# Placement of the experts' weights merged into routing, and parts of 16, 24 and 24 tiles

## What is computed

```python
logits = jnp.einsum('btd,ed->bte', x, gate_w) + expert_bias      # 12 experts
topk_logits, topk_idx = jax.lax.top_k(logits, TOP_K)             # TOP_K = 2
topk_w = jax.nn.softmax(topk_logits, axis=-1)
w = jnp.einsum('btk,btke->bte', topk_w, onehot)
w_zero = jnp.sum(w[..., E_FFN:], axis=-1)                        # experts 8 to 11 return x
h = jax.nn.silu(jnp.einsum('btd,efd->btef', x, w1))              # 8 experts, 256 -> 512
y = jnp.einsum('btef,edf->bted', h, w2)                          # 512 -> 256
out = jnp.einsum('bte,bted->btd', w_ffn, y) + w_zero[..., None] * x
```

## Time and profile before

| what | value |
|---|---|
| median of 3 runs | 2664.8 us |
| the profiled execution | 2638.58 us |
| its span | 2636.6 us |
| PE busy | 2485.2 us (94%) |
| DVE, ACT, POOL busy | 1906.8, 1665.0, 767.3 us |
| routing, first to last instruction | 1967.9 to 2106.1 |
| placement | 2109.2 to 2146.1 |
| experts | 2146.5 to 2636.6 |
| output scatters (L1998) | 122 |

### The profile page before, as it was taken

The page is one execution under the profiler, slowest core; times in us unless marked ns, Lnnn a source line. Parts: engine busy times, 40 slices in busy tenths (PEclk is TensorE's granted clock), DMA queues, the critical chain, the costliest instruction groups (busy, mean ns, idle before and its releaser), DMA issues. The chain is left out here.

```text
span 2636.6 us, 47763 instructions
## 1 busy us (share of the span) xinstructions
PE 2485.2 (94%) x16108; PEld 1295.4 (49%) x16109; DVE 1906.8 (72%) x3228; ACT 1665.0 (63%) x2989; POOL 767.3 (29%) x896
## 2 busy tenths in 40 slices
PE   6987789999999999999999999999989779999998
PEld 4554223333333333333333333333338669989997
DVE  5887768888788887787887887878818655556543
ACT  1656347777777777777777777777765355545554
POOL 2545301121111111111211111111113747757644
PEclk8999779999999999999999999999999789999999
DMA  5698643242442432433424323321128457567565
GB/s 176 200 255 220 132 81 87 67 112 82 94 90 75 98 91 74 100 86 81 86 83 91 88 79 78 70 54 38 54 70 256 161 172 138 114 107 130 95 102 76
DMA packets 225081, 286.06 MB, mean 108 GB/s; under 512 B 29526, under 2 KB 178550, under 8 KB 224502
## 3 DMA queue, kind: packets, MB, share of 16 engines
q1 hardware_dynamic: 185596, 235.80, 35.6%
q0 software_dynamic: 32160, 41.57, 9.2%
q10 hardware_dynamic: 7136, 6.32, 0.7%
HBM read 143.64 MB, written 139.08 MB: 107 GB/s over the span
## 5 line engine op out<-in xcount | busy, mean ns | idle before, releaser
L240 DVE TENSOR_REDUCE mxc<-ps 128x2 f32<-128x1024 f32 (+4 forms) x1168 | 1298.0, 1149 | 316.2 <-PE ps L228 165.8
L1188 ACT ACTIVATE probs<-ps 128x512 f32<-128x512 f32 (+1 forms) x2240 | 1177.6, 588 | 462.2 <-PE ps L1145 450.6
L1161 PE MATMUL ps<-probs,vs 128*32 128x512 f32 (+3 forms) x5120 | 599.7, 541 | 1.3 <-POOL probs L1078 1.2
L1145 PE MATMUL ps<-qs,ks 99*128 99x512 bf16 (+3 forms) x1760 | 504.5, 352 | 14.0 <-DMA qs<-m_t 9.2
L228 PE MATMUL ps<-ks,qs 96*128 96x512 bf16 (+3 forms) x1760 | 464.5, 354 | 25.2 <-DVE mxc L240 17.4
L1078 POOL TENSOR_SCALAR_AFFINE_SELECT probs<-probs 128x512 f32<-128x512 f32 x256 | 161.7, 635 | 869.3 <-ACT probs L1188 869.3
L1145 PEld LDWEIGHTS ps<-qs,ks 99*128 99x128 bf16 x1760 | 147.5, 97 | 380.3 <-ACT probs L1188 271.7
L228 PEld LDWEIGHTS ps<-ks,qs 96*128 96x128 bf16 x1760 | 163.3, 99 | 178.8 <-DVE mxc L240 42.6
L1874 PEld LDWEIGHTS ps<-x_t,w_at 128*128 128x128 f32 x2000 | 245.1, 194 | 11.7 <-issue 5.6
L1874 PE MATMUL ps<-x_t,w_at 128*128 128x128 f32 x2000 | 246.6, 277 | 4.2 <-ACT x_t L1915 4.2
L1998 POOL DMA_INDIRECT out<-ys,idx x122 | 194.6, 1595 | 172.7 <-DMA out<-ys,idx 91.5
(11 more groups left out here) (172 smaller groups left out, 2206.4 us busy)
## 6 DMA issues: line engine op xcount, KB each, us to landing
ks<-k_parts SPq DMA_DIRECT2D x66, 256.0 KB, 4.2
qs<-q_parts SPq DMA_DIRECT2D x66, 256.0 KB, 4.1
xs<-slot_x SPq DMA_DIRECT2D x128, 131.0 KB, 2.2
v_ones<-vout SPq DMA_DIRECT2D x64, 256.0 KB, 3.6
vs<-v_ones SPq DMA_DIRECT2D x64, 256.0 KB, 3.2
attn_t<-o_sb SPq DMA_DIRECT2D x64, 256.0 KB, 2.8
slot_x<-zero SPq DMA_DIRECT2D x48, 262.0 KB, 2.5
q_parts<-parts SPq DMA_DIRECT2D x96, 128.0 KB
```

Of the source, the lines that this page charges most:

```text
L240: return dve.tensor_reduce(mxc[:, h0:h0 + nh, i, c], unit_view(ps, u, at), AX_X, ALU.max)
L1145: ins = pe.matmul(o[:, h, :], ks[r][0:SROWS + MROWS, h0 + h, j * P:(j + 1) * P], qs[r][0:SROWS + MROWS, h0 + h, J * QJ + lo:(J + 1) * QJ], ...
L1161: ins = pe.matmul(o_ps[SLOT * g:SLOT * (g + 1), lo:QJ], vs[:, r, j, SLOT * g:SLOT * (g + 1)], probs[:, (NKT * r + m) % NPB, g, 0:QJ - lo], ...
L1188: act.activation(probs[:, (NKT * r + m) % NPB, h0:h0 + nh, 0:QJ - lo], st_view(r, s), ACT.Exp, scale=DH ** -0.5).then_inc(exp_done, 1)
```

## The change

- `PARTS` is 16, 24, 24. NPAIR becomes 20, 28, 28, and part 0 lies in one batch, part 2 in two.
- `place` is gone. Its work stands in `route`'s lists: part 0's chain in steps 8 and 9, part 1's in steps 16 and 17, part 2's in steps 20 and 21 (its counts stand ahead of the transposes of expert 5), the transposes and copies of expert e in step 16 + e, the loads of experts 2 to 7 at the end of SyncE's list, the tile tables at the end of VectorE's.
- All chains share one set of buffers (`chain_buffers`); `positions` multiplies in place and reduces in two instructions. The counts of a later part wait until the one before is placed.
- POOL scatters in each of the last 8 steps of routing, two in the first four and three in the others, and then all the rest of part 0 and the first 6 tiles (`AHEAD`) of part 1. `later` of part 0 in the experts is shorter by these 6.
- `rbc` is one buffer, so the load of group t waits for the multiply of group t - 1.

```diff
-PARTS = [24, 24, 16]
+PARTS = [16, 24, 24]
-SCATTERING = 6
-EARLY = 14
+SCATTERING = 8
+AHEAD = 6
...
 class Chain:
-        self.sel, self.posf, self.slot = sb("sel", [P, 2, n, E]), sb("posf", [P, 2, n]), sb("slot", [P, 2, n])
+        self.posf, self.slot = (view(x, 2 * n, "p (c t) -> p c t", c=2) for x in ("posf", "slot"))
...
     def positions(self, dve, s, r, pos_done):
         for c in range(2):
-            s.mark(dve.tensor_tensor(self.sel[:, c, :, :], rank, self.oh[:, c, :, 0:E], ALU.mult))
+            s.mark(dve.tensor_tensor(self.oh[:, c, :, 0:E], rank, self.oh[:, c, :, 0:E], ALU.mult))
         s.wait()
-        s.link(dve.tensor_reduce(self.posf[:, :, :], self.sel[:, :, :, :], AX_X, ALU.add))
+        for c in range(2):
+            s.mark(dve.tensor_reduce(self.posf[:, c, :], self.oh[:, c, :, 0:E], AX_X, ALU.add))
+        s.wait()
...
 def route
-                        if t >= RAW + 2:
-                            sp.wait_ge(y_done, t - RAW - 1)
+                        if t > RAW:
+                            sp.wait_ge(y_done, t - RAW)
...
+                for e in range(2, E):
+                    for m in range(2):
+                        sp.wait_ge(wt_done, 4 * (e - 2) + 2 * (m + 1))
+                        load_weights(sp, a, w_in, w_ld, e, m)
...
+                def counts(*parts):
+                    def stage(t):
+                        for p in parts:
+                            if t == LASTS[p]:
+                                pe.wait_ge(oh_done, p + 1)
+                                if p > 0:
+                                    pe.wait_ge(pos_done, 2 * p)
+                                chains[p].counts(pe, r, bank).then_inc(cnt_mm, 1)
+                def weights(t):
+                    e = t - (NB - E)
+                    for half in range(4):
+                        m, h, n = half // 2, half % 2, 4 * e + half
+                        if h == 0:
+                            pe.wait_ge(w_ld[m][e % 2], 16 * (e // 2 + 1))
+                        if n == 0:
+                            pe.wait_ge(mid_done, NB)
+                        if n >= 4:
+                            pe.wait_ge(wt_copy, n - 3)
...
-                blocks((6, counts), (0, output), (3, logits), (2, normed))
+                blocks((6, counts(0, 2)), (8, counts(1)), (0, output), (3, logits), (8, weights), (2, normed))
...
-                blocks((2, scales), (3, shifted), (5, top2), (0, attended), (1, residual), (4, inverses), (4, table), (5, chosen), (6, placed), (9, zeros))
+                blocks((2, scales), (3, shifted), (5, top2), (0, attended), (1, residual), (4, inverses), (4, table),
+                       (5, chosen(0, 2)), (6, placed(0, 2)), (7, zeros), (7, chosen(1)), (8, placed(1)))
                 dve.wait_ge(topi_done, NB)
+                dve.wait_ge(mult_done, NB)
+                for p in range(NPARTS):
+                    tile_table(dve, s, r, p, cmp, eidf, last, turned)
...
-                blocks((1, deviation), (1, normalise), (2, normed), (5, shares))
+                blocks((1, deviation), (1, normalise), (5, shares(0, 2)), (8, shares(1)), (8, weights), (2, normed))
...
-                todo = [(t, c) for t in range(PARTS[0]) for c in range(2)]
+                todo = [(t, c) for t in range(PARTS[0] + AHEAD) for c in range(2)]
...
-                        for _ in range(3):
-                            scatter_row(pool, d, r, *todo.pop(0), scat)
+                        for _ in range(2 if t < NB - SCATTERING // 2 else 3):
+                            scatter()
                 blocks((0, modulate), (0, scatters))
-                while len(todo) > 2 * (PARTS[0] - EARLY):
-                    scatter_row(pool, d, r, *todo.pop(0), scat)
+                while todo:
+                    scatter()
+                scattered(pool, 0, scat[0])
...
-def place(nc, a, k, r, w, w_in, w_ld, d, ps, scat):
...
 def experts
-        later = [range(FIRST[p + 1], FIRST[p + 1] + PARTS[p + 1]) if p + 1 < NPARTS else range(0) for p in range(NPARTS)]
+        later = [range(FIRST[p + 1] + (AHEAD if p == 0 else 0), FIRST[p + 1] + PARTS[p + 1]) if p + 1 < NPARTS else range(0) for p in range(NPARTS)]
```

More of the change, by code:

```diff
@@ L1433, in route @@
         HK = H // KC
-        chain = Chain(ctx, nc, 0, PARTS[0])
+        bufs = chain_buffers(ctx, nc)
+        chains = [Chain(ctx, nc, bufs, p) for p in range(NPARTS)]
+        cmp, eidf = hn[:, :, :].rearrange("p j c -> p (j c)")[:, 0:HT * E].rearrange("p (t e) -> p t e", e=E), sb("eidf_all", [P, HT])
+        last, turned = sb("last", [P, 1]), sb("turned_at", [P, HT])
+        wt_done, wt_copy = sem("wtr"), sem("wtc")
         c_ld, cstep, oh_done, cnt_mm, pos_done, w_dif, w_sig = (sem(n) for n in ("c", "cstep", "oh", "cnt", "pos", "dif", "sig"))
@@ new lines, in placed, with stage @@
+                def placed(*parts):
+                    def stage(t):
+                        for p in parts:
+                            if t == LASTS[p]:
+                                dve.wait_ge(cnt_mm, p + 1)
+                                chains[p].ranks(dve, s, r, bank)
+                                chains[p].positions(dve, s, r, pos_done)
+                                dve.wait_ge(w_sig, p + 1)
+                                chains[p].extras(dve, s, r)
+                                dve.nop().then_inc(pos_done, 1)
+                                if p > 0:
+                                    chains[p].zero_weights(dve, s, r)
+                    return stage
@@ L1646, in normed, with shares, stage, weights @@
                     act.copy(h2_t[:, :, :, :], pd).then_inc(ht_done, 1)
[L1648 to L1653 removed]
+                def shares(*parts):
+                    def stage(t):
+                        for p in parts:
+                            if t == LASTS[p]:
+                                act.wait_ge(w_dif, p + 1)
+                                chains[p].shares(act, r, w_sig)
+                    return stage
+                def weights(t):
+                    e = t - (NB - E)
+                    if e < 0:
+                        return
+                    for half in range(4):
+                        m, h = half // 2, half % 2
+                        act.wait_ge(wt_done, 4 * e + half + 1)
+                        dst = w["w1t"][:, e, h, :] if m == 0 else w["w2t"][:, e, 2 * h:2 * h + 2, :].rearrange("p f c -> p (f c)")
+                        act.copy(dst, ps[:, half, :]).then_inc(wt_copy, 1)
+                blocks((1, deviation), (1, normalise), (5, shares(0, 2)), (8, shares(1)), (8, weights), (2, normed))
             @block.gpsimd
@@ L1775, in experts @@
-def experts(nc, d, k, r, w, zb, ps, out):
+def experts(nc, d, k, r, w, zb, ps, out, scat):
     with ExitStack() as ctx:
```

174 lines of the change are left out of this document (57 added, 117 removed).

## The result

The changed kernel takes **2679.64 us** (median of 10 runs, 2674.85 to 2683.0), the kernel before beside it 2665.96 (10 runs): ratio 1.0045, 95% interval 1.0033 to 1.0058. Between the medians lie 13.7 us (by the ratio 12.0), slower, and 2679.6 is outside the forecast range of 2651 to 2673. The profiled execution took 2674.85 us.

The account below looks back on a forecast made before the run. In the end of routing no engine is full, so the order of queues counts; TensorE fills the experts. Tail -11 and part 0 +9 give -2, with the first steps -2.5: 2664.8 to about 2662 us, range 2651 to 2673.

Parts of the forecast that it names:

- I work out the difference in the profiled execution and carry it over to the median.: Whole kernel: difference worked out on the 2638.6 us profiled execution, then applied to the 2664.8 us median, 26.2 above it.
- The term of the merged tail: End of routing with placement: VectorE's tile tables end it at 2134.9 instead of ScalarE's copy at 2146.1, 11 us gained.
- the single buffer of inverses: Routing steps 0 to 15: the load's wait costs nothing, 3 us as other bound; steps some 2.5 us earlier.
- The term of part 0: Experts: POOL sends part 1's rows too late for the shortened part 0, TensorE waits, 9 us lost.
- The budget of POOL: Part 0 of the experts: POOL's scatters, additions and waits sum to 124.7 us until the word for part 1.
- no loss, as now: Experts, change from part 1 to 2: POOL's word comes before TensorE ends, so nothing is lost.
- would be 25: Experts, part 0: the loss without the six tiles sent ahead, which save 15.5 us of POOL's queue.
- The tail at full clock: Rival, end of routing: transposes fill TensorE's pauses, full clock, end near 2128, 18 gained, total 2656; chance 0.24.
- POOL not late in part 0: Rival, experts: waits and scatters overlap better, loss 0 to 1 us, total 2654; chance 0.10.
- POOL's waits at even changes: Rival, part 0 of the experts: expert changes at even tiles also wait 2.65 us, 10.6 more, total 2673; chance 0.12.
- The weights ending the stage: Rival, end of routing: weight loads still end it, near 2142, only 4 us gained, total 2669; chance 0.12.
- the 0.18 for slower: Whole kernel: chance given to a time above 2670.1 us, mostly from late POOL waits and weights ending routing.

Follow-up runs that it names:

- e1: The kernel before, unchanged, run again for a second profile: 2668.1 us, ratio 1.0006.
- e8: The changed kernel, with POOL holding back the last 24 scatters of routing until ScalarE has copied the weights: 2689.4 us, ratio 1.0091.
- e5: The changed kernel with FLIGHT = 1, a tile's scatters waiting until the tile before has landed: 2685.1 us, ratio 1.0076.
- e6: The kernel before with FLIGHT = 1, a tile's scatters waiting until the tile before has landed: 2690.7 us, ratio 1.0091.
- e17: The kernel before with 24 row scatters repeated in part 2, on a chip with late signals: 2668.5 us, ratio 1.0031.
- e9: The kernel before with 24 row scatters repeated in part 2, on a chip without late signals: 2645.1 us, ratio 1.0021.
- e10: The kernel before, sending row scatters always two tiles in a pair, in groups of four, on a chip without late signals: 2650.4 us, ratio 1.0045.
- e13: The changed kernel, unchanged, on a chip without late signals: 2647.3 us, ratio 1.0032.
- e15: The kernel before with only routing and placement merged, old part sizes, on a chip without late signals: 2631.5 us, ratio 0.9972.
- e7: The changed kernel with 12 tiles of part 1 sent ahead in routing instead of 6: 2683.3 us, ratio 1.0068.
- e14: The kernel before with only the part sizes 16, 24, 24, on a chip without late signals: 2657.9 us, ratio 1.0073.
- e2: The changed kernel, unchanged, run again for a second profile: 2682.8 us, ratio 1.0058.
- e3: The kernel before with only the part sizes 16, 24, 24, on a chip with late signals: 2679.9 us, ratio 1.0043.
- e4: The kernel before with only routing and placement merged, old part sizes, on a chip with late signals: 2669.5 us, ratio 1.0013.

## Why the prediction was wrong

Forecast was -2.5 us, measured are +13.7. Of these 16.2 us about 5 come from late signals, 6 from terms of the sum that were mis-sized or put at nothing, and 5 are open.

**The first step that failed: "I work out the difference in the profiled execution and carry it over to the median."** The 26.2 us between them were read as a constant. By all that the runs show they were late signals: the profile has none and the time of the chips without them (2638.6; 2638 to 2640 in the runs above), the timed runs have the time of the others (2662 to 2666). And what e1 takes more than the profile of before lies only where POOL scatters rows: 10.8 us in the stage, then, from the first product with w2 to the last, 179.3 instead of 162.5 in part 0 and 172.1 instead of 170.2 in part 1; part 2, which scatters none, takes 117.6 in both. Each chip was seen at one time only, so whether it is lasting stays open.

The tail that the merge builds is the most exposed place of the kernel: TensorE, ScalarE and VectorE hand over to one another while POOL scatters without pause. The stage of the changed kernel grows from 171.7 to 190.2 and 190.8, that of the kernel before from 180.7 to 191.5. So of the merge's gain of 9 us 1 is left. That this is scatters against signals is shown by taking them away (e8; e5 and e6 too, at a price) and by putting them where there were none (e17, against e9); e10 shows that it takes the chip as well.

**The term of the merged tail, -11 us:** on e13 the stage's end is the last table, 2135.9, 168.9 us after the start of routing (before: ScalarE's copy at 178.2): 9.3 gained. From POOL's last multiply to there it is 50.9 us, and the forecast's (2084.0 to 2134.9) is 50.9 too. The order of the queues, what ends the stage and the 27 scatters beside it (done at 2123.8, forecast 2120) were right. That the sum agrees to the tenth is luck: the transposes of expert 0, for one, took 3.6 us, not 2.7.

**A term put at nothing: the single buffer of inverses.** The first steps came 0.6 us earlier and not 2.5. The prediction gave the load of inverses "a landing of some 3" and the stores of x_mid "2 us of slack". In the profile of before that load lands after 5.4 us (median), and what costs is not the load but what stands behind it in SyncE's queue:

```profile
2045.22 0.51 SPq L1476 DMA_DIRECT2D rbc<-rden  x1
...
2046.41 0.51 SPq L1482 DMA_DIRECT2D out<-x_midb  x1
...
2054.61 1.23 DVE L1607 TENSOR_TENSOR x_midb<-ps,shared 128x1024 f32<-128x1024 f32 x1 [2.73 <-DMA out<-x_midb]
```

On e13 the x_mid of group 10 was ready at 2039.2, but SyncE stood until 2045.2 with the load that waits for the multiply of the step before, and stored it at 2046.41; the residual of group 12, which writes the same half of the buffer, then waited 2.73 us. The kernel before stored group 10 at once (2036.64). VectorE waits for such stores in all 11 profiles of kernels with one buffer, 2.9 to 6.1 us in each, and in none of the 9 with two. (The 2.5 us are in the forecast's 2134.9 already; the step of the sum from -2 to -2.5 counts part of them twice.)

The granted clock of that tail lay between forecast and rival (its second half; the second row is the change to part 2, of which below):

```profile
2106.00:2136.00 30.00, 19.80 (x128) 17.64 (x127) 14.92 (x74) 15.37 (x29) 13.33 (x14) 0.84 0.70 242
2447.00:2460.00 13.00, 9.43 (x47) 8.43 (x46) 6.53 (x24) 5.88 (x9) 6.24 (x4) 0.74 0.49 74
```

**The term of part 0, +9 us, measured 12.7** (experts 488.0 to 500.7). The budget of POOL was right: from its first addition to the word 123.4 us (2150.09 to 2273.53, where SyncE loads), forecast 124.7. The gap between the last product and the first was 17.9 (2266.88 to 2284.80), forecast 20.5: 6.8 above before, not 9.4. But two losses beside it were put at nothing. TensorE's part 0 took 2.4 us longer than 12 tiles less (its last product ends 116.8 after POOL's first addition, forecast 114.4), 1.8 of it waiting for a ys that POOL had not yet taken: a full queue delays its own additions before it delays the word. And the change to part 2, called "no loss, as now", took 11.1 us (2447.29 to 2458.39) instead of 8.0: after an idle time of 2.40 us the first two sets of sixteen products took 2.73 and 3.75 us, at a granted clock of 0.74 in that stretch (last row above). The kernel before idled 1.66 us there and stayed at 1.00:

```profile
2503.00 2.02 PE L1874 MATMUL ps<-x_t,w_at 128*128 128x128 f32 x16 [0.81 <-ACT x_t L1915]
...
2498.00:2511.00 13.00, 9.71 (x69) 8.55 (x68) 5.41 (x26) 7.04 (x11) 3.30 (x2) 1.00 0.33 58
```

The length of the idle time does not decide this, as the other profiles show. The same 1.66 us in e15 were followed by sixteen products in 3.49 us,

```profile
2500.61 3.49 PE L1872 MATMUL ps<-x_t,w_at 128*128 128x128 f32 x16 [0.91 <-ACT x_t L1913]
```

and 2.45 and 2.58 us in e7 and e14 by 2.02. In the other profiles of the changed kernel (after, e2) this change took 10.0 and 9.9 us, in those of the kernel before as it was (e1) 8.0, and in e9, the same up to there, 9.4; so part of the 3.1 us is the chance of one execution.

Sum: 6.8 + 2.4 + 3.1 = 12.3 of 12.7; the rest is part 0's first tiles (8.1 us from the first transposes to the first product with w2, before 7.7). The estimate that without the six tiles ahead the loss "would be 25" is e14: 512.9 - 488.0 = 24.9. There the number is better than the mechanism: the gap grew by 11.0 (22.1 against 11.1), and part 0 itself, where the forecast had nothing, took 13.5 longer than 12 tiles less.

**Together**, without late signals, -9.0 + 12.7 = +3.7 (less 0.9 of an earlier start: spans 2636.6 and 2639.4), where the forecast had -2.5. The medians there differ by 8.9; e13's profiled execution was the shortest of its eight (2641.47, median 2647.3), and what the others spend more has no profile: open. The mechanisms of both terms held, but their sizes turned the sign of the sum. By the medians (+8.9 there, +13.7 in the result) the late signals added 5 us; the intervals of the two ratios overlap, and on chip A the change cost 16.4.

**The rivals.** The tail at full clock (2656): on e13 the granted clock was 0.66 from 2084 to 2106 and 0.84 behind it (0.50 and 0.80 in the old stretches), and the end came at 2135.9, not 2128. The rule of the Trainium skill that the prediction set against the trace ("TensorE: Matmul & The Clock Gate", Part 1: activity releases the clock) is borne out in part by this trace, and the end of the tail came no earlier than forecast. POOL not late in part 0: refuted, it was. POOL's waits at even changes: its budget came out without them. The weights ending the stage: no, 2132.2 in e13. None of them was a signal held up, so the 0.18 for slower had the wrong reason behind it.

## What to carry to other kernels

Where one profiled execution lies well off the median of the runs, ask what the others have that it has not before a sum is built on it; here the 1% between them was a whole mechanism. Work moved into a stretch where three engines hand over to one another pays only if nothing beside it delays the hand-overs, and a POOL queue of indirect scatters can be such a thing on some chips. A part's work and what must be sent for the next part have to shrink together: a queue that was exactly full (44 tiles, 48 scatters) is late with 32 tiles and 36. One buffer less can put a wait into an ordered queue, and then it is worth asking what stands behind that wait, not only what waits.

## What the runs showed of the hardware

- Chips differ: the kernel before took 2639.5 and 2638.4 on two and 2666.4, 2665.8 and 2661.7 on three others, 0.9 to 1.1%.
- On the slower ones a signal of TensorE to ScalarE, VectorE and SyncE comes about 2 to 20 us after the records show its work done, while POOL sends indirect row scatters 1.27 us apart; behind groups of four 26 of 29 times, of two 10 of 72 (after, e1, e3). In e4 and e7 the last ones held came 5.1 and 5.2 us behind POOL's last scatter. Where the signal is held, the runs do not show.
- A wait for a late signal has its own mark: "remote" in the timeline of a kernel with one core, and "another core or an unknown queue" in the chain.
- Where the experts change part, an idle time of 1.66 to 2.58 us can be followed by half clock or not: sixteen products took 2.02 us after 1.66 (before), 2.45 (e7) and 2.58 us (e14), and 3.49 after 1.66 (e15) and 2.73, then 3.75, after 2.40 (e13).
